# One 128-column transpose and four small shift DMAs for a group's row maxima; stack loads three groups ahead

## The reference

```python
q, k, v = split_heads(x @ Wq), split_heads(ctx @ Wk), split_heads(ctx @ Wv)   # 16 heads of 16
scores  = einsum('bhqd,bhkd->bhqk', q, k) / sqrt(16)                          # 512 x 512 a head
attn    = softmax(scores, axis=-1)
out     = einsum('bhqk,bhkd->bhqd', attn, v) @ Wo
```

## Time and profile before

| | |
|---|---|
| median of 3 runs | 1280.65 us (1279.75 to 1281.99) |
| the profiled execution | 1274.43 us, its span 1272.7 us |
| TensorE busy | 1131.4 us, 89% |
| VectorE, ScalarE, GpSimd busy | 66%, 52%, 17% |
| TensorE's granted clock | 0.949 of full speed |
| DMA | 139.40 MB, mean 110 GB/s |

### The profile page before, as it was taken

The page is one execution under the profiler, slowest core; times in us unless marked ns, Lnnn a source line. Parts: engine busy times, 40 slices in busy tenths (PEclk is TensorE's granted clock), DMA queues, the critical chain, the costliest instruction groups (busy, mean ns, idle before and its releaser), DMA issues. The chain is left out here.

```text
span 1272.7 us, 17810 instructions
## 1 busy us (share of the span) xinstructions
PE 1131.4 (89%) x5693; PEld 544.0 (43%) x5722; DVE 838.6 (66%) x2112; ACT 660.4 (52%) x1341; POOL 210.9 (17%) x272
## 2 busy tenths in 40 slices
PE   7889999999997999999967999996989999998390
PEld 4423343434453223343364666664523333335370
DVE  5878777777478888888762222223888888876722
ACT  3346666666533677677722333332537767674250
POOL 4310000000143000000202222211520010102154
PEclk9989999999999899999967999998989999999795
DMA  8953321221048433543291140103873323211064
GB/s 265 309 169 93 79 57 28 81 52 26 2 154 291 103 91 90 132 97 93 72 375 33 31 161 28 27 13 102 263 241 91 90 59 89 60 37 57 25 171 144
DMA packets 100706, 139.40 MB, mean 110 GB/s; under 512 B 8452, under 2 KB 82632, under 8 KB 99208
## 3 DMA queue, kind: packets, MB, share of 16 engines
q1 hardware_dynamic: 96536, 128.03, 33.6%
q0 software_dynamic: 4080, 10.23, 2.9%
HBM read 86.30 MB, written 52.17 MB: 109 GB/s over the span
## 5 line engine op out<-in xcount | busy, mean ns | idle before, releaser
L885 ACT ACTIVATE r<-ps 128x512 f32<-128x512 f32 x768 | 427.4, 600 | 211.9 <-PE ps L971 122.1
L377 DVE TENSOR_REDUCE m<-ps 128x1 f32<-128x512 f32 x512 | 320.9, 682 | 45.2 <-PE ps L958 44.9
L971 PE MATMUL ps<-r 99*128 99x512 bf16 x768 | 294.3, 388 | 5.6 <-ACT r L885 5.6
L958 PE MATMUL ps<-r 96*128 96x512 bf16 x720 | 280.9, 393 | 20.5 <-DVE m L377 7.0
L373 DVE CUSTOM_DVE_ANT_0 r<-ps,r 128x512 bf16<-128x512 f32 x256 | 170.2, 690 | 60.2 <-PE ps L958 59.6
L985 PE MATMUL ps<-r 128*32 128x512 f32 x1536 | 204.9, 605 | 4.9 <-ACT r L885 3.3
L971 PEld LDWEIGHTS ps<-r 99*128 99x128 bf16 x768 | 74.4, 98 | 211.7 <-ACT r L885 157.3
L958 PEld LDWEIGHTS ps<-r 96*128 96x128 bf16 x720 | 71.3, 99 | 105.9 <-DVE m L377 24.3
L861 POOL COPY r<-r 128x256 f32<-128x256 f32 x48 | 19.0, 399 | 542.1 <-PE ps L985 542.1
L1660 DVE COPY r<-ps 128x512 f32<-128x512 f32 x46 | 31.8, 691 | 91.9 <-PE ps L1707 91.9
L1707 PE MATMUL ps<-r 128*128 x184 | 87.8, 621 | 2.7 <-issue 0.4
(11 more groups left out here) (151 smaller groups left out, 1220.5 us busy)
## 6 DMA issues: line engine op xcount, KB each, us to landing
r<-q_parts SPq DMA_DIRECT2D x48, 384.0 KB, 5.2
r<-k_parts SPq DMA_DIRECT2D x48, 384.0 KB, 6.0
k_parts<-r SPq DMA_DIRECT2D x24, 384.0 KB, 3.3
q_parts<-r SPq DMA_DIRECT2D x24, 384.0 KB, 3.1
r<-in_w SPq DMA_DIRECT2D x16, 512.0 KB, 4.9
r<-in_w SPq DMA_DIRECT2D x8, 1024.0 KB, 14.4
k_parts<-r SPq DMA_DIRECT2D x24, 256.0 KB, 3.3
q_parts<-r SPq DMA_DIRECT2D x24, 256.0 KB, 3.1
```

Of the source, the lines that this page charges most:

```text
L377: ins = dve.tensor_reduce(out, mem.ps[:, bank, :], AX.X, ALU.max)
L885: act.activation(mem.probs[:, u // HG, u % HG, :], ps[:, ST + (UNITS * g + u) % DEEP, :], ACT.Exp, scale=SCALE).then_inc(a.p_exp.sem, 1)
L958: pe.matmul(ps[:, led_bank(n), :], mem.qst[g][0:ROWS, h, t * P:(t + 1) * P], mem.kst[g][0:ROWS, h, :], start=True, stop=True).then_inc(a.s ...
L971: ins = pe.matmul(out, mem.kst[g][0:KROWS, h, kt * P:(kt + 1) * P], mem.qst[g][0:KROWS, h, :], start=True, stop=not a.masked)
```

## The change

- `mparts` becomes one 128 x 128 tile whose first 48 columns hold the parts of all four query tiles, tile by tile; the rest is zero, set once by a new memset among the constants (so `setup` counts to 14).
- `maxima` is one transpose of the whole tile: 128 weight columns, 128 rows of output.
- ScalarE copies 48 x 128 instead of 12 x 512; `mT` has that shape.
- `shift` is four DMAs, one for each query tile, each from 12 rows of `mT` to a 128-column piece of the three rows of `qst[g]`; its semaphore counts 64 a batch instead of 16.
- `AHEAD = 3`: three groups' stacks instead of two are loaded in the opening, and in group G the stacks of group G + 3, once group G - 1 is through. That is when group G begins, before the shift of group G + 1.

```diff
--- before.py
+++ after.py
@@ -98,8 +98,8 @@
         self.rstd_g = sb("rstd_g", [P, B, T])
         self.m = sb("m", [P, T, HG])
         self.mres = sb("mres", [P, T, HG])
-        self.mparts = sb("mparts", [P, T, PARTS, HG], BF16)
-        self.mT = sb("mT", [PARTS * HG, S], BF16)
+        self.mparts = sb("mparts", [P, P], BF16)
+        self.mT = sb("mT", [PARTS * T * HG, P], BF16)
         self.den = sb("den", [P, T, HG])
         self.rden = sb("rden", [P, T, HG])
 
@@ -262,7 +262,7 @@
             self.shift_ones = sig("shift_ones", 16)
 
         self.stacks = [sig(f"stacks{s}", 32) for s in range(NG)]
-        self.shift = [sig(f"shift{s}", 16) for s in range(NG)]
+        self.shift = [sig(f"shift{s}", 16 * T) for s in range(NG)]
         self.s_ps = sig("s_ps", UNITS)
         self.s_max = sig("s_max", UNITS)
         self.cut = sig("cut", CUTS)
@@ -713,7 +713,7 @@
     def rest_of_batches():
         context(1)
         if a.fresh:
-            sp.wait_ge(a.setup, 13)
+            sp.wait_ge(a.setup, 14)
             for s in range(NG):
                 sp.dma_start(mem.kst[s][ROWS:KROWS, :, :].rearrange("r h (i n) -> r (h i) n", n=P),
                              mem.ones[0:PARTS, :].unsqueeze(1).to_broadcast([PARTS, HG * S // P, P]))\
@@ -724,8 +724,8 @@
             body(b, b + 2)
         for n in range(QK):
             sp.wait_ge(a.stored[n].sem, a.stored[n].at(1))
-        load_stacks(sp, a, 0, 0)
-        load_stacks(sp, a, 0, 1)
+        for g in range(AHEAD):
+            load_stacks(sp, a, 0, g)
         body(B - 2, None)
         body(B - 1, None)
 
@@ -754,6 +754,7 @@
 HALF_TURN = (3, 13)
 LAST_TURN, LAST_OUT = (5, 2), (3, 4)
 LATE = 2
+AHEAD = 3
 
 M_STEP, TURN_STEP = 8, 12
 OUT_TURNS = (3, 5)
@@ -789,18 +790,20 @@
 
         G = NG * b + g
         sp.wait_ge(a.m_sb.sem, a.m_sb.at(G, 1))
-        sp.dma_start(mem.qst[g][ROWS:KROWS, :, :], mem.mT[:, :]).then_inc(a.shift[g].sem, 16)
+        for t in range(T):
+            sp.dma_start(mem.qst[g][ROWS:KROWS, :, t * P:(t + 1) * P],
+                         mem.mT[t * PARTS * HG:(t + 1) * PARTS * HG, :]).then_inc(a.shift[g].sem, 16)
 
     def body(b, first, last):
         for g in range(NG):
             G = NG * b + g
-            ahead = (b, g + 2) if g < 2 else (b + 1, g - 2)
-            if not (last and g >= 2):
-                if first and g == 2:
+            ahead = (b, g + AHEAD) if g + AHEAD < NG else (b + 1, g + AHEAD - NG)
+            if not (last and g + AHEAD >= NG):
+                if first and g + AHEAD == NG:
                     for n in range(QK):
                         sp.wait_ge(a.stored[n].sem, a.stored[n].at(B))
-                if not (first and g < 2):
-                    sp.wait_ge(a.st_ps.sem, a.st_ps.at(G - 1))
+                if G + AHEAD >= NG:
+                    sp.wait_ge(a.st_ps.sem, a.st_ps.at(G + AHEAD - NG + 1))
                 load_stacks(sp, a, *ahead)
             if a.self_block and g == OUT_TILES[-1][0] and not first:
                 store(b - 1)
@@ -894,8 +897,8 @@
         act.wait_ge(a.m_ps.sem, a.m_ps.at(G, 1))
         if used is not None:
             b, g = used
-            act.wait_ge(a.shift[g].sem, a.shift[g].at(b, 16))
-        act.activation(mem.mT[:, :], ps[0:PARTS * HG, MISC, 0:S // 2].bitcast(BF16), ACT.Copy)\
+            act.wait_ge(a.shift[g].sem, a.shift[g].at(b, 16 * T))
+        act.activation(mem.mT[:, :], ps[0:PARTS * T * HG, MISC, 0:P // 2].bitcast(BF16), ACT.Copy)\
            .then_inc(a.m_sb.sem, 1)
 
     def mask_copy(b, i, bank=MISC):
@@ -964,7 +967,7 @@
             used = before(b, UNITS * g + u)
             pe.wait_ge(a.p_exp.sem, a.p_exp.at(used[0], used[1] + 1))
         if u == 0:
-            pe.wait_ge(a.shift[g].sem, a.shift[g].at(b, 16))
+            pe.wait_ge(a.shift[g].sem, a.shift[g].at(b, 16 * T))
             if a.masked and g == 0:
                 pe.wait_ge(a.mbT_ready.sem, a.mbT_ready.at(b, MASK_ROUNDS))
         out = ps[:, ST + (UNITS * g + u) % DEEP, :]
@@ -989,10 +992,7 @@
     def maxima(G):
         pe.wait_ge(a.cut.sem, a.cut.at(G, CUTS))
         take_misc()
-        for t in range(T):
-            ins = pe.transpose(ps[0:PARTS * HG, MISC, t * P // 2:(t + 1) * P // 2].bitcast(BF16),
-                               mem.mparts[:, t, :, :].rearrange("p a h -> p (a h)"), mem.identb[:, :])
-        ins.then_inc(a.m_ps.sem, 1)
+        pe.transpose(ps[:, MISC, 0:P // 2].bitcast(BF16), mem.mparts[:, :], mem.identb[:, :]).then_inc(a.m_ps.sem, 1)
         misc[0] = (a.m_sb.sem, a.m_sb.at(G, 1))
 
     def turn_mask(b, i, bank=MISC):
@@ -1121,7 +1121,8 @@
         if not (type(G) is int and G < 1):
             dve.wait_ge(a.m_ps.sem, a.m_ps.at(G))
         m = mem.m[:, :, :]
-        hi, mid, lo = (mem.mparts[:, :, i, :] for i in range(PARTS))
+        mparts = mem.mparts[:, 0:T * PARTS * HG].rearrange("p (t a h) -> p t a h", t=T, a=PARTS)
+        hi, mid, lo = (mparts[:, :, i, :] for i in range(PARTS))
         dve.tensor_scalar(hi, m, -1.0, None, ALU.mult).then_inc(a.cut.sem, 1)
         dve.wait_ge(a.cut.sem, a.cut.at(G, 1))
         dve.scalar_tensor_tensor(mem.mres[:, :, :], m, -1.0, hi, ALU.mult, ALU.subtract).then_inc(a.cut.sem, 1)
@@ -1876,10 +1877,11 @@
             pool.memset(mem.identb[:, :], 0.0).then_inc(setup, 1)
             pool.memset(mem.ones[:, :], 1.0).then_inc(setup, 1)
             pool.memset(mem.tri[:, :], 1.0).then_inc(setup, 1)
+            pool.memset(mem.mparts[:, :], 0.0).then_inc(setup, 1)
             pool.memset(mem.onehot[:, NT, :], 0.0).then_inc(setup, 1)
             pool.iota(mem.count_i[:, :], [[1, P]], base=0, channel_multiplier=0).then_inc(setup, 1)
             pool.iota(mem.number_i[:, :], [[1, 1]], base=0, channel_multiplier=1).then_inc(setup, 1)
-            pool.wait_ge(setup, 8)
+            pool.wait_ge(setup, 9)
             for eye in (mem.ident, mem.identb):
                 pool.affine_select(out=eye[:, :], in_=eye[:, :], compare_op=ALU.not_equal, fill=1.0, base=0,
                                    pattern=[[-1, P]], channel_multiplier=1).then_inc(setup, 1)
@@ -2014,7 +2016,7 @@
 
             @block.tensor
             def _(pe):
-                pe.wait_ge(setup, 13)
+                pe.wait_ge(setup, 14)
                 begin, rest = project_tensor(pe, xa0)
                 begin()
                 pe.wait_ge(weights_a, 32)
```

## The result

The changed kernel takes 1271.13 us (median of 5 runs, 1269.85 to 1271.86) beside 1279.75 us for the kernel before (median of 5, 1277.08 to 1281.99): a ratio of 0.9933 with a 95% interval of 0.9918 to 0.9948, so 8.6 us faster. The forecast was 1264.6 us, 16.0 us faster; the measured time lies just above the range. Two executions of the experiments that ran far slower than the others (2287 and 1378 us) are in no median and no ratio. The two profiled executions differ by only 3.3 us (1271.13 against 1274.43), since that of the kernel before lay 5 us under its median.

The account below looks back on a forecast made before the run. TensorE's instruction order was taken to bound most of the attention stages. Terms -14.6 - 5.0 + 1.1 + 2.5 = -16.0 us gave 1258.4 us, carried to the median as 1264.6; 8-in-10 range 1258 to 1271 us.

Parts of the forecast that it names:

- The transposes: In TensorE's attention stages, one 128-column transpose replaces four narrow ones, saving 0.34 us in an ordinary group, -14.6 us in all.
- The copy: ScalarE's copy to mT falls from 577 to about 300 ns, worth nothing by itself; the shift starts 0.27 us earlier.
- The four shifts: On SP, the last of four lands at 3.9, at most 4.1 us; PE waits only in two last groups, +1.1 us.
- rival 1: Each shift DMA waits for the one before to land, so PE waits in the unmasked groups: +25 us, 1305 us; chance 0.06.
- The stack waits: TensorE's waits for stack loads in the attention loops all go under the new load order: -5.0 us.
- Rival 4: Waits for stacks only hid another wait just behind, so that term gives 0: -11.0 us, 1269.7 us; chance 0.10.
- PE's saving: TensorE's saved time in the attention stages gets through, as ScalarE idles 0.77 us and VectorE 0.79 us after such a block.
- Rival 2: VectorE or ScalarE takes up PE's saving and sets the pace: only -1.4 us is left, 1279.2 us; chance 0.06.
- The openings: A third pair of stack loads ahead of stores costs +2.0, 0 and +0.5 us in the three stages, together +2.5.
- Rival 3: Extra loads cost full price in all three openings and hold back more than themselves: 7.2 us, giving 1269.3 us; chance 0.12.
- the two signs: The forecast is wrong if the last shift lands later than 5 us or the wide transpose isn't near 0.06 us.
- its worst ends: All terms at their least favourable bounds: -10.2 - 4.7 + 1.5 + 4.8 = -8.6 us, giving 1272.0 us.

Follow-up runs that it names:

- the edit alone: Kernel before, with only group 2's stack loads put in each opening and left out at group 0, old order otherwise: 1283.39 us, ratio 1.0076.

## Why the prediction was half right

**The transposes: right.** Forecast -14.6 us. The block is 0.28 us, the figure forecast, and the 45 blocks in the loops give 14.8 us. From the new load order with old transposes (0.9967) to the same with new ones (0.9841) it is -16.1 us, transposes and shifts together, against -14.6 + 1.1 = -13.5; the loops of the two profiles give 653.9 - 639.9 = 14.0. The reason was incomplete: the prediction gave the 0.08 us ahead of the first transpose to the narrow form and 0.27 us to three instructions fewer, whereas 0.20 us are the full width, whose load is hidden, and 0.15 the fewer instructions.

**The copy: right.** 264 ns against 300, worth nothing by itself.

**The four shifts: right in their timing, and rival 1 falls.** Their issues take 2.94 us, 0.74 each, and unit 0 follows the first by 1138.91 - 1134.79 = 4.1 us in the last group:

```profile
1134.79 2.94 SPq L794 DMA_DIRECT2D r<-mT  x4
...
1138.91 0.59 PE L974 MATMUL ps<-r 99*128 99x512 bf16 x2 [0.56 <-ACT r L888]
```

The bracket names ScalarE; that the shift is what ends this wait is seen from its absence with one shift. Forecast was a last landing at 3.9, at most 4.1. The wait of 0.55 us is there (the gap is 0.95 us where it was 0.22, so 0.73), but the last group is 0.6 us shorter after it (11.05 against 11.66), so +1.1 was nearer to 0. Ordinary groups don't wait: there unit 0 comes 4.46 us or more behind the issue, which is a margin of 0.3 us, not a wide one.

**The stack waits: right within the error.** Forecast -5.0; -4.2 measured (2.5 to 5.7). Rival 4, that they only hide others, falls.

**PE's saving gets through.** Rival 2 would have left 1.4 us; with the openings' cost taken away the kernel gains 20.3 us.

**The openings: the step that failed.** The prediction put it: "+2.0" for the first stage, "In the second stage SP rests ... and covers most of the two issues: 0", "In the third ... +0.5", together "+2.5, between 0 and 4.8". Measured by adding the edit alone it is +9.7 us, by the load order with and without it 10.8, by taking it out of the changed kernel 11.6, each within some 3 us; the openings of the profiles grow by 8 to 12 us together. The size of the transfer was about right, 2.3 to 2.7 us of added wait a pair in the first opening of one series of profiles. Three things were not. The second and third opening were excused, the one by SP's free issue time, which is no room in the DMA engines, the other by ScalarE's wait being "the first stage's alone": a row that shows no wait before shows no margin either. (With two pairs, three other profiles do show a wait of 5.2 to 5.8 us in the third opening.) One wait became six, 4.8 us became 27.6, because the stores behind the loads are late in each opening. And where TensorE ran out of work, the granted clock fell, for 6.8 us in the changed kernel. Such an extra spell of 3.4 to 10.2 us, 16 to 23 us before the end of an opening, is in all five profiles with an early third pair (once in each of the changed kernel, twice with the load order alone and with the edit alone, in all three openings with four pairs) and in none of the eight without. Rival 3 named the right mechanism, but its 7.2 us, thrice the transfer, is still too low: it had nothing for the clock.

**Its own signs and bounds.** Neither of the two signs that it named for being wrong came: the last shift landed before 5 us and the wide transpose is at 0.06 us. They watched the terms that held. The sign that did come was in its list all the same, ScalarE's wait in the first opening "near 6 us", which is 8.14. That the sum of its worst ends is -8.6 us, the measured gain, is luck: the transposes came in full, and the openings cost at least twice their worst end of 4.8. Two of its chances are also off by 0.01: the parts add up to 0.86 faster and 0.08 slower.

**The balance.** -16.1 (transposes, shifts) - 4.2 (stack waits) + 9.7 to 11.6 (openings) = -8.7 to -10.6 us, and -8.6 was measured. With 11.6 the sum closes by itself, since it comes from the same runs; the test is the 9.7 of the edit alone, which leaves 2 us, within the error.

## What to carry to other kernels

A load issued early is paid for by what is queued behind it: before moving a transfer ahead of stores, look for the instruction that waits for those stores to free a buffer, in each stage where they meet, and ask there whether the DMA engines have room, not whether the queue has free issue time. Here the place of two DMAs a stage cost more than half of what the rest of the change gained (11.6 of 20.3 us), and putting the pair behind the first shift gives 1253.66 us, 1.6% under the kernel before; none of the versions tried here can be told to be faster. For a small bf16 transpose between large matmuls it is worth trying all 128 columns, even if most hold zeros: here it was cheaper than 48, because its load was hidden.

## What the runs showed of the hardware that was not expected

- A bf16 transpose with 48 weight columns costs 0.48 us in a stream of matmuls 0.22 us apart, one with 128 columns 0.28, at equal load durations (99 and 98 ns). The 128-column load starts a median of 0.22 us ahead of its matmul, the 48-column load with it. It was shown for this one place, 48 times in a run, not for a row of such instructions.
- Four SBUF to SBUF DMAs of 3 KB, issued back to back, take 2.94 us on SP, and TensorE goes on 4.13 us after the first issue. One alone has its packets moved 1.6 us after its issue begins, so four in series would need 6.4: they overlap.
- In the openings, where the DMA engines are full (share 1.07 to 1.12), the first six `k_parts` issues of the first opening take 6.49 to 8.69 us behind three pairs of loads and 4.91 to 5.55 behind two, once 6.34: a full DMA system is seen in the duration of later issues on the same queue.
- TensorE without work for 3.25 us was followed by 6.8 us at the lower clock level, in the other profile of the changed kernel 3.49 us by 6.8 as well; with four pairs 6.75 us idle go with a spell of 10.2. Every kernel with an early third pair has such a spell in some opening and the others have none; but an idle time of 2.05 us had none, and that the idle time itself brings the spell was not tried apart.
